# One 28-block transposing transfer per chunk with two staging buffers, in place of 8 and 20 blocks with one, and the last norms apart

## The reference

```python
state = x
for _ in range(5):
    s_in, s_out = state @ in_W.T + in_b, state @ out_W.T + out_b
    a_in, a_out = adj @ s_in, adj.T @ s_out          # 2048x2048, entries 0 or 1
    a = concatenate([a_in, a_out, state])            # 768 features
    r = sigmoid(a @ r_W.T + r_b)
    z = sigmoid(a @ z_W.T + z_b)
    h = tanh(concatenate([a_in, a_out, r * state]) @ h_W.T + h_b)
    state = (1 - z) * state + z * h
out = layernorm(x + tanh(state @ o1_W.T + o1_b) @ o2_W.T + o2_b)
```

## Time and profile before

| | us |
|---|---|
| median of 3 runs | 1041.88 (1041.09 to 1047.54) |
| the profiled execution's own time | 1042.67 |
| its span in the profile | 1040.9 |
| TensorE busy | 1006.7 (97%) |
| VectorE busy | 592.3 (57%) |
| ScalarE busy | 399.6 (38%) |
| hardware DMA queue, share of 16 engines | 35.5% |

### The profile page before, as it was taken

How to read it: one execution, slowest core, us unless ns; L and a number is a source line. 1 busy time by engine, 2 the same in 40 slices (tenths; PEclk the granted TensorE clock), 3 DMA queues, 4 the chain that set the end, 5 groups by cost and what they waited for, 6 DMA issues and landing times.

```text
span 1040.9 us, 11449 instructions
## 1 busy us (share of the span) xinstructions
PE 1006.7 (97%) x4648; PEld 456.8 (44%) x4648; DVE 592.3 (57%) x936; ACT 399.6 (38%) x539; POOL 37.9 (4%) x43
## 2 busy tenths in 40 slices
PE   7999999999999999999999999999998999999994
PEld 3444444444444444444444444444443444444442
DVE  5999868995353346544433565353346534446756
ACT  3655665542153135313411552152144314322442
POOL 0311000000000000000000000000000002101100
PEclk9999999999999999999999999999999999999998
DMA  9999991336420343333004533410344335001101
GB/s 342 363 393 388 379 325 31 76 80 208 169 106 1 142 151 61 71 142 142 1 1 156 173 61 94 170 56 0 142 152 67 66 142 187 1 1 41 41 1 41
DMA packets 87236, 134.30 MB, mean 129 GB/s; under 512 B 60432, under 2 KB 75408, under 8 KB 78992
## 3 DMA queue, kind: packets, MB, share of 16 engines
q1 hardware_dynamic: 84336, 124.67, 35.5%
q0 software_dynamic: 2304, 8.39, 2.0%
q10 hardware_dynamic: 544, 0.52, 0.1%
HBM read 102.11 MB, written 16.78 MB: 114 GB/s over the span
## 4 chain that ended last, share of the span: by engine, by line
PE 76%; DMA 10%; ACT 6%; DVE 4%; issue 2%; SPq 1%; ACTq 0%; DVEq 0%
PE bank L1221 38%; PE bank L1134 36%; DMA tmp<-in_adj_t 4%; DMA tmp<-in_adj 4%; ACT areg L405 3%; DMA xop_words<-pq_words 2%; PE bank L1234 1%; ACT tmp L456 1%; DVE pq_words L787 1%; PE bank L1077 1%; PE bank L1253 1%; ACT pq_words L448 1%; ACT split L431 1%; DVE tmp L831 0%; DVE bank L808 0%
## 5 line engine op out<-in xcount | busy, mean ns | idle before, releaser
L1134 PE MATMUL bank<-areg,xop_words 128*128 128x512 fp8e4 x1792 | 390.2, 379 | 1.3 <-DVE pq_words L973 0.9
L1221 PE MATMUL bank<-pq_words,w 128*128 128x512 f16 x1440 | 328.4, 380 | 0.0
L1134 PEld LDWEIGHTS bank<-areg,xop_words 128*128 128x128 f16 x1792 | 174.3, 98 | 214.7 <-DVE pq_words L973 3.0
L1221 PEld LDWEIGHTS bank<-pq_words,w 128*128 128x128 f16 x1440 | 141.3, 98 | 171.3 <-issue 2.5
L456 ACT ACTIVATE tmp<-bank,bias_sb,scal 128x512 f32<-128x512 f32 x120 | 92.9, 774 | 178.3 <-PE bank L1221 178.3
L1221 PE MATMUL bank<-split,w 128*128 128x512 f16 x480 | 118.8, 384 | 9.5 <-DVE bank L808 7.6
L534 ACT ACTIVATE pq_words<-pq_words 128x512 f16<-128x512 f32 x48 | 30.2, 629 | 236.8 <-DVE pq_words L985 140.5
L808 DVE SCALAR_TENSOR_TENSOR bank<-deg_words,vdeg,bank 128x512 f32<-128x512 f16 x120 | 90.0, 752 | 48.8 <-ACT bank L470 47.7
L1077 PE MATMUL bank<-areg,xop_words 128*128 128x512 fp8e4 x512 | 112.6, 379 | 5.3 <-ACT areg L405 4.5
L470 ACT ACTIVATE bank<-deg_words,vdeg 128x512 f32<-128x512 f16 x120 | 82.7, 691 | 5.3 <-DVE deg_words L772 1.6
L1077 PEld LDWEIGHTS bank<-areg,xop_words 128*128 128x128 f16 x512 | 49.3, 98 | 68.0 <-issue 7.4
(11 more groups left out here) (119 smaller groups left out, 598.4 us busy)
## 6 DMA issues: line engine op xcount, KB each, us to landing
areg<-kept_operands SPq DMA_DIRECT2D x32, 1792.0 KB, 10.6
tmp<-in_adj SPq DMA_DIRECT2D x16, 1024.0 KB, 7.8
tmp<-in_adj_t SPq DMA_DIRECT2D x16, 1024.0 KB, 8.5
kept_operands<-xop_words POOLq DMA_DIRECT2D x11, 512.0 KB, 8.2
areg<-in_x SPq DMA_DIRECT2D x8, 512.0 KB, 7.7
kept_operands<-areg SPq DMA_DIRECT2D x4, 1024.0 KB, 9.1
kept_operands<-tmp POOLq DMA_DIRECT2D x5, 512.0 KB, 3.3
pq_words<-in_gate_w SPq DMA_DIRECT2D x6, 384.0 KB, 5.5
```

The lines of the kernel that those rows point to most:

```text
L1134: last = nc.tensor.matmul(dst[:, :], xop[:, m // 2, operand_block(xo, part, m % 2), :], slot8[g % 2][:, m, mo, :], start=first and m == pa ...
L1221: last = nc.tensor.matmul(dst[:, :], w16[:, k, wp, feat(gi)], rhs, start=False, stop=i == KT - 1 and (wp, xp) == PASSES[-1], skip_group_ch ...
```

## The change

Three things change. (1) A chunk is turned with one transposing transfer of all 28 blocks, issued when the second piece is staged. (2) There are two staging buffers, `turn_slots`: the old place, and a second in `tmp` (the words of `ring_b`, in use for other data during step 0). Chunks with n < 4 all use the first; later ones alternate. `rows_hi(n, 0)` waits only for the last transfer out of its own buffer. TensorE waits for whole chunks: for chunk 2 at the start of `first_group`, and for chunk 3 after four early products instead of three (XS4 early is moved ahead). (3) At the end the statistics of chunk 2 are finished before the residual of chunk 3. The residual of chunk 2 is cut in two halves around the last `head_split`; the inverse root is a `Sqrt` on ScalarE, a reciprocal and one Newton round on VectorE, once for chunk 2 and once for chunk 3. ScalarE normalises the four row tiles of chunk 2 and two of chunk 3, VectorE the other two of chunk 3, and SyncE issues all stores.

```diff
-        turn = pq_words[:, 0:NX * 2 * P].bitcast(F16)
+        turn_slots = [w.bitcast(F16) for w in (pq_words[:, 0:NX * 2 * P], tmp[:, 8 * CW:8 * CW + NX * 2 * P])]
...
+        def turn_slot(n):
+            return 0 if n < CH else n % 2
+
+        def turns(n, b):
+            return len([i for i in range(n + 1) if turn_slot(i) == b])
+
+        def wait_turned(eng, n):
+            for b in range(2):
+                need(eng, s_turn[b], 16 * turns(n, b))
...
             def turn_rows(n):
-                for f in range(2):
-                    sp.wait_ge(s_xl, 2 * n + f + 1)
...
-                    bs = turn_blocks[f]
-                    sp.dma_start(xop[:, n % CH, bs, :], turn[:, bs.start * P:bs.stop * P], transpose=True) \
-                        .then_inc(s_turn[f], 16)
+                sp.wait_ge(s_xl, 2 * n + 2)
...
+                sp.dma_start(xop[:, n % CH, :, :], turn_slots[turn_slot(n)], transpose=True) \
+                    .then_inc(s_turn[turn_slot(n)], 16)
...
             def rows_hi(n, f):
+                turn = turn_slots[turn_slot(n)]
                 if f == 0:
                     act.wait_ge(s_new, FT * n + 1)
-                    for part in range(2):
-                        need(act, s_turn[part], 16 * n)
+                    need(act, s_turn[turn_slot(n)], 16 * turns(n - 1, turn_slot(n)))
...
-            for h in range(2):
-                for j in (2 * h, 2 * h + 1):
-                    act.wait_ge(s_rstd, 1)
-                    nc.scalar.activation(y[:, 0, j, :], y[:, 0, j, :], ACT.Identity, scale=ln_t[:, 3, j:j + 1],
-                                         bias=ln_t[:, 4, j:j + 1]).then_inc(s_norm_a, 1)
-                act.wait_ge(s_norm_a, 2 * h + 2)
-                nc.scalar.dma_start(out.rearrange("(j p) f -> p j f", p=P)[:, 2 * JC + 2 * h:2 * JC + 2 * h + 2, :],
-                                    y[:, 0, 2 * h:2 * h + 2, :]).then_inc(s_out[0], 16)
+            for part, c, js in ((0, CH - 2, range(JC)), (1, CH - 1, range(JC // 2, JC))):
+                act.wait_ge(s_var, part + 1)
+                nc.scalar.activation(ln_t[:, 5, part * JC:(part + 1) * JC], ln_t[:, 0, part * JC:(part + 1) * JC],
+                                     ACT.Sqrt).then_inc(s_root, 1)
+                act.wait_ge(s_rstd, part + 1)
+                for j in js:
+                    at = part * JC + j
+                    nc.scalar.activation(y[:, c % 2, j, :], y[:, c % 2, j, :], ACT.Identity, scale=ln_t[:, 3, at:at + 1],
+                                         bias=ln_t[:, 4, at:at + 1]).then_inc(s_norm_a, 1)
...
+            def inverse_root_by_act(part):
+                js = slice(part * JC, (part + 1) * JC)
+                var, a, b, r, mr, root = [ln_t[:, i, js] for i in range(6)]
+                nc.vector.tensor_scalar(var, ln_mv[:, js, 1], LN_EPS, None, ALU.add).then_inc(s_var, 1)
+                dve.wait_ge(s_var, part + 1)
+                dve.wait_ge(s_root, part + 1)
+                ln_link(nc.vector.reciprocal(r, root))
+                ln_link(nc.vector.tensor_tensor(a, r, r, ALU.mult))
+                ln_link(nc.vector.scalar_tensor_tensor(b, a, -0.5, var, ALU.mult, ALU.mult))
+                ln_link(nc.vector.scalar_tensor_tensor(r, b, 1.5, r, ALU.add, ALU.mult))
+                nc.vector.scalar_tensor_tensor(mr, ln_mv[:, js, 0], -1.0, r, ALU.mult, ALU.mult).then_inc(s_rstd, 1)
...
-            residual(2)
+            residual_rows(2, range(JC // 2))
             head_split(CH - 1)
+            residual_rows(2, range(JC // 2, JC))
             aggregate(range(JC))
+            inverse_root_by_act(0)
             residual(CH - 1)
             aggregate(range(JC, 2 * JC))
-            inverse_root(2 * JC)
-            nc.vector.scalar_tensor_tensor(ln_t[:, 4, :], ln_mv[:, :, 0], -1.0, ln_t[:, 3, :], ALU.mult, ALU.mult) \
-                .then_inc(s_rstd, 1)
-            normalize(CH - 1, JC)
+            inverse_root_by_act(1)
+            normalize(CH - 1, JC, range(JC // 2))
...
             def first_group(t):
-                pe.wait_ge(s_turn[0], 16 * n)
+                wait_turned(pe, n - 1)
                 product(bank_a, g, X11, M11, early, final=False)
                 need(pe, s_y21, at)
-                pe.wait_ge(s_turn[1], 16 * n)
                 product(bank_b, g, XS2, MT2, early, final=False)
                 need(pe, s_u4, at)
                 product(bank_e, g, XS1, MT1, early, final=False)
-                pe.wait_ge(s_turn[0], 16 * (n + 1))
-                product(bank_a, g, X11, M11, late, first=False).then_inc(s_p1, 1)
                 need(pe, s_y12, at)
                 product(bank_c, g, XS4, M22, early, final=False)
+                wait_turned(pe, n)
+                product(bank_a, g, X11, M11, late, first=False).then_inc(s_p1, 1)
+                product(bank_b, g, XS2, MT2, late, first=False).then_inc(s_p6, 1)
                 pe.wait_ge(s_sum1, at + 1)
                 product(bank_a, g, X12, M21, every, first=False).then_inc(s_p2, 1)
-                pe.wait_ge(s_turn[1], 16 * (n + 1))
-                product(bank_b, g, XS2, MT2, late, first=False).then_inc(s_p6, 1)
                 product(bank_e, g, XS1, MT1, late, first=False).then_inc(s_p5, 1)
```

More of the change, by code:

```diff
@@ L134, in gnn_program @@
         ln_mv = sb("ln_mv", [P, 2 * JC, 2], F32)
-        ln_t = sb("ln_t", [P, 5, 2 * JC], F32)
+        ln_t = sb("ln_t", [P, 6, 2 * JC], F32)
         PX, SIG, PW, OMG, OMGP, UG, UO1, UO2, OM1, OM2, T0, T1, SIGX = [scal[:, i:i + 1] for i in range(13)]
@@ L175, in gnn_program @@
         s_sph, s_spl = sem("s_sph"), sem("s_spl")
-        s_turn = [sem("s_turn0"), sem("s_turn1")]
+        s_turn = [sem(f"s_turn{b}") for b in range(2)]
         s_xs, s_xc, s_xh, s_xl = sem("s_xs"), sem("s_xc"), sem("s_xh"), sem("s_xl")
@@ L179, in gnn_program @@
         s_o2, s_y, s_ln, s_norm = sem("s_o2"), sem("s_y"), sem("s_ln"), sem("s_norm")
-        s_rstd, s_norm_a = sem("s_rstd"), sem("s_norm_a")
+        s_var, s_root, s_rstd, s_norm_a = sem("s_var"), sem("s_root"), sem("s_rstd"), sem("s_norm_a")
         s_finh, s_finl = sem("s_finh"), sem("s_finl")
@@ L236, in store_rows @@
             for h in range(2):
-                sp.wait_ge(s_norm, JC * min(c, 2) + 2 * h + 2)
+                if c < 2 or (c == CH - 1 and h == 0):
+                    sp.wait_ge(s_norm, JC * min(c, 2) + 2 * h + 2)
+                else:
+                    sp.wait_ge(s_norm_a, 2 * h + 2 if c == 2 else JC + 2)
                 sp.dma_start(out.rearrange("(j p) f -> p j f", p=P)[:, c * JC + 2 * h:c * JC + 2 * h + 2, :],
@@ L298, in turn_rows @@
             def turn_rows(n):
-                for f in range(2):
-                    sp.wait_ge(s_xl, 2 * n + f + 1)
[L301 to L306, removed]
-                    bs = turn_blocks[f]
-                    sp.dma_start(xop[:, n % CH, bs, :], turn[:, bs.start * P:bs.stop * P], transpose=True) \
-                        .then_inc(s_turn[f], 16)
+                sp.wait_ge(s_xl, 2 * n + 2)
+                need(sp, s_p4, 4 * (n // CH))
+                if n == 0:
+                    sp.wait_ge(s_p0, 2 * CH)
+                    for i in range(3):
+                        sp.wait_ge(s_kept_a[i], 16 * len(range(i, RING_A, 3)))
+                sp.dma_start(xop[:, n % CH, :, :], turn_slots[turn_slot(n)], transpose=True) \
+                    .then_inc(s_turn[turn_slot(n)], 16)
             store_raw(0)
@@ L347, in _ @@
                     store_rows(sp, c - 1)
+            store_rows(sp, CH - 2)
             store_rows(sp, CH - 1)
@@ L436, in rows_hi @@
                 new = state_t[:, :, cols(c)]
+                turn = turn_slots[turn_slot(n)]
                 if f == 0:
                     act.wait_ge(s_new, FT * n + 1)
-                    for part in range(2):
-                        need(act, s_turn[part], 16 * n)
+                    need(act, s_turn[turn_slot(n)], 16 * turns(n - 1, turn_slot(n)))
+                    if n == CH + 1:
+                        for i in range(2):
+                            act.wait_ge(s_kept_b[i], 16 * len(range(i, GATE_JOBS, 2)))
                     nc.scalar.activation(turn[:, 0:4 * P], new[:, 0, :], ACT.Identity, scale=SIGX).then_inc(s_xh, 1)
@@ L926, in statistics, with residual_rows @@
                 return nc.vector.bn_stats(ln_st[:, (JC if c == CH - 1 else 0) + j, :], y[:, c % 2, j, :])
-            def residual(c):
+            def residual_rows(c, js):
                 dve.wait_ge(s_xb, c + 1)
-                for j in range(JC):
+                for i, j in enumerate(js):
                     if c == CH - 1 or j % 2 == 0:
@@ L935, in residual @@
                         .then_inc(s_y, 1)
-                    if j > 0:
-                        statistics(c, j - 1)
-                ln_link(statistics(c, JC - 1))
+                    if i > 0:
+                        statistics(c, js[i - 1])
+                ln_link(statistics(c, js[-1]))
+            def residual(c):
```

(9 more changed lines are left out.)

1 line of the change is left out of this document (removed).

## The result

| | before | changed |
|---|---|---|
| median of 6 runs, us | 1042.95 (1041.09 to 1047.54) | 1053.31 (1048.88 to 1054.29) |
| the profiled execution | 1042.67 | 1054.13 |
| its span | 1040.9 | 1052.3 |

The ratio of changed to before is 1.0091, with a 95% interval of 1.0067 to 1.0115: slower, by somewhat more than the 0.7% forecast. The median is 4.3 us above the 1049.0 predicted. That is inside the range of 1040 to 1057, and 1.3 above the 1046 to 1052 that the prediction gave the forecast itself.

The account below looks back on a forecast made before the run. TensorE, busy 97% of the span, was taken as the bound. Costs 5.6 + 8.2 + 5.1 less gains 7.1, 3.1 and 1.6 gave +7.1 on 1042.67, less 0.8: 1049.0 us, range 1040 to 1057.

Parts of the forecast that it names:

- the forecast itself: The case that the whole sum holds, 1049.0 us, with 1046 to 1052 as its own range; chance 0.38.
- The second buffer: Gates of steps 1 to 3: three waits for degree_part go, 7.1 us, and slow stretches behind two of them, 3.1.
- The length of the transfer: A 28-block transfer lands 6.0 us after issue, from 3.0 for 8 blocks and 4.8 for 20.
- 28 blocks for the price of 20: Rival: the whole transfer takes 4.8 us, idle times at the first groups shrink, time 1041 us; chance 0.1.
- a longer transfer: Rival: each us above 6.0 costs 5 us in all, 1054.5 us at 7.1; chance 0.17.
- The starts of the first groups: After the gates TensorE idles 3.2 us for chunk 2, 3.3 more in step 1; cost 5.6 there, 8.2 in steps 2 to 4.
- The wait for the sum: Before XS3 in the first group: TensorE's 0.4 us wait for VectorE's sum vanishes, covered by 20 matmuls.
- The clock: Four of five new idle times at the first groups bring 1.2 GHz, three at 1.7 us each: 5.1 us.
- The fourth stretch at 0.50: Sign: the clock view has four stretches at 0.50, as four of the five new idle times were expected to bring.
- The end: Behind the last matmuls: new order and Sqrt let the last store issue at 1036.5, not 1038.12; gain 1.6 us.

Follow-up runs that it names:

- the first experiment: The changed kernel with each chunk sent as 8 and 20 blocks again and the old order of first_group, two buffers and new end kept: 1029.62 us, ratio 0.9885.
- the one with two whole chunks: The kernel with two transfers, two buffers and the new end, but chunks 0 and 1 of each step sent whole: 1029.28 us, ratio 0.9878.
- the later wait: The changed kernel with the early products of chunks 0 and 1 of all four banks put ahead of the wait for chunk 2: 1050.26 us, ratio 1.0084.
- The experiment with more cover: The changed kernel with XS4 late put ahead of TensorE's wait for VectorE's sum: 1054.44 us, ratio 1.0117.

## Why the prediction was right, and where it was off

**The second buffer** removed the three large waits and their slow stretches: forecast 10.2 us, measured 10.3 by the medians (11.0 by the ratio) with the second buffer alone.

**The length of the transfer**, 6.0 forecast from two rows, was 6.1. The rivals that rested on it, 28 blocks for the price of 20 and a longer transfer, fall.

**The starts of the first groups**: 3.2 us idle at each, measured 3.2 to 3.3; 3.3 more in step 1, measured 2.88; chunk 3 covered in steps 2 to 4, as it was. The five waits have 15.9 us in all where the forecast had 16. That the late landing is the loss, and neither the buffer nor whole transfers where nobody waits for them, is shown by the first experiment and by the one with two whole chunks; that moving the wait helps little, by the later wait. The first transfer of a chunk overlaps with staging, and the merged one starts later than it and ends later than the 20-block one, 6.1 us after staging and not 4.8. The Trainium skill ("DMA: Bandwidth & Descriptors", Rules for kernel authors) has the rule to coalesce many small transfers, and calls those under 64 KB mostly overhead. The rows agree that there is a fixed cost, 1.8 us, but the smaller transfer here has 256 KB (8 blocks of 128 x 128 f16), and saving its fixed cost made this kernel slower.

**The wait for the sum** is the step that failed. The prediction counted "a wait for VectorE's sum, which the new order covers with 20 matmuls", from the end of XS2 late. But VectorE's list has the low part of y11 (L1032) ahead of the sum (L1006). It needs the high part from ScalarE (L548), and that needs the end of X12. Step 2 in the changed kernel:

```profile
450.86 0.60 ACT L548 ACTIVATE pq_words<-bank 128x512 f16<-128x512 f32 x1 [3.73 <-PE bank L1167]
451.49 0.69 DVE L1032 SCALAR_TENSOR_TENSOR pq_words<-bank,pq_words 128x512 f16<-128x512 f32 x1 [15.06 <-ACT pq_words L548]
452.10 0.68 DVE L1006 TENSOR_TENSOR pq_words<-bank,pq_words 128x512 f32<-128x512 f32 x1
```

From the first row to XS3 at 452.84 it is 2.0 us, and it was 2.0 before (440.92 to 442.90). Between the end of X12 and XS3 there were 8 matmuls before and there are 4 now, 0.86 us less. So the wait went from 0.29 us (the sum took 0.4 for it) to 1.15 instead of to nothing: 4 x 1.15 = 4.6 us over the forecast, most of the 6.2 that the table is short of. The experiment with more cover bears this out.

**The clock**: four of the five new idle times were expected to be followed by the slow clock, three of them at a cost of 1.7 each, 5.1. Three were followed by it, those of steps 2 to 4, with 6.4 us in all, since the first was about twice as long; neither of step 1 was. The fourth stretch at 0.50, which the prediction counts among its signs, stands in the last `head_out`, where the forecast had none. So the price is short by 1.3, and that three costly stretches came, as forecast, is partly luck. Over the six runs of the changed kernel the time went from 1048.88 us at a mean granted clock of 0.994 to 1054.29 at 0.986, so part of the spread goes with the clock; where the streaming stage ends spreads it too, and no run here tells how much each gives.

**The end**: 1.6 forecast, 1.5 measured, with Sqrt at 0.20 us and 0.3 until VectorE went on, and the table load in ScalarE's idle time. The last residual was forecast at 1030.4, 60.3 us after the last gates, and started 60.3 after them. That the last `head_out` would be held up for 3.3 us by the moved half of the residual I had overlooked; in the profile of the changed kernel it cost nothing, in five others with the same end 0.7 to 1.0 us.

**Some luck in the number.** The parts after the first gates cost 13.2 us and not 7.0, nearly twice. In the time the miss looks smaller, +10.4 by the medians (9.5 by the ratio) for +7.1, and in the two profiles 1.8 us of the miss is hidden by step 0, which took that much less though nothing in it was edited.

## What to carry to other kernels

Before two transfers are merged, ask which block of them is wanted first and last, and by whom: the merged one can't start before the last block is ready nor be used before the last has landed; the fixed cost saved, here 1.8 us, did not make up for that. A wait is covered by the work between the end of what the waiting chain really hangs on and its use; find that from the order of the engine that does the sum, and when matmuls are moved to cover one wait, look at which wait they covered till then. Two edits of one change can pull against each other, here by +22 and -10 us: try them apart.

## What the runs showed of the hardware

A transposing transfer from SBUF to SBUF costs 1.8 us and 0.15 us for each 128 x 128 f16 block over 8 to 28 blocks (3.0, 4.8, 6.1 us), and its issue takes 1.2, 3.0 and 4.2 us of the queue.

After idle times of 2.0 to 3.3 us between unbroken matmuls the granted clock of TensorE was often, not always, 0.50 for a while. In step 1 of the changed kernel idle times of 3.16 and 2.88 us were not followed by it; in step 1 of the kernel with more cover for the sum one of 3.17 was (the 48 matmuls behind it took 12.21 us, not 10.52). The kernel before shows it after two of its three large waits. The kernel with only the new end has the same waits and shows it after all three (stretches behind each; busy us of the engines, then clock, DMA, GB/s):

```profile
405.00:408.00 3.00, 3.00 (x8) 1.03 (x7) 2.96 (x5) 1.43 (x3) 0.00 (x0) 0.50 0.00 0
600.00:603.00 3.00, 3.00 (x9) 1.02 (x7) 3.00 (x5) 0.80 (x2) 0.00 (x0) 0.52 0.00 0
795.00:797.00 2.00, 2.00 (x6) 0.70 (x5) 2.00 (x4) 1.19 (x2) 0.00 (x0) 0.50 0.00 0
```

With two transfers and two buffers no such wait is left from the first gates on, and the clock stays at 1.00 up to 1000 us, shortly before the last head:

```profile
137.00:400.00 263.00, 262.02 (x1211) 118.08 (x1212) 157.68 (x223) 104.10 (x145) 3.63 (x5) 1.00 0.36 119
400.00:800.00 400.00, 399.43 (x1850) 180.50 (x1849) 196.99 (x295) 144.02 (x201) 0.00 (x0) 1.00 0.30 95
800.00:1000.00 200.00, 199.71 (x950) 92.54 (x948) 104.39 (x185) 65.58 (x90) 15.73 (x16) 1.00 0.19 62
```

What decides whether an idle time is followed by the slow clock was not tried.
